# Token rows stored as 16-bit halves and transposed by their load DMAs, in a mixture-of-experts kernel

## The chip, the core and the metric

The kernel runs on one core of a Trainium2 chip. The metric is the time of one execution in microseconds (us) of device time; the median of several executions counts. TensorE (PE) multiplies matrices out of the on-chip memory SBUF into the accumulator memory PSUM, in tiles of 128 partitions. VectorE (DVE), ScalarE (ACT) and GpSimd (POOL) do the elementwise work; SyncE (SP) here issues DMAs, and GpSimd issues the indirect ones, which scatter rows to addresses that a table holds. Sixteen DMA engines serve all queues. Engines run side by side, each through its own list of instructions in order, and wait for each other by semaphores.

## What is computed

x has 2 x 1024 tokens of 256 values. The first half of the reference is a cross attention in three rounds with the tokens as slots; the second is a mixture of experts with routing, and the change lies there:

```python
x = x + _L0_xcond_ref(cond_1024, ctx_1024, _layernorm(x), ...)
x = x + _L0_ffn_ref(_layernorm(x), ...)

# _L0_ffn_ref: E = 32 experts, H = 256, I = 128, TOPK = 8
scores = jax.nn.sigmoid(h @ gate_w.T)
# the 8 best experts of 4 of 8 groups, weights normalised and scaled by 2.5
combine = (jax.nn.one_hot(tki, E) * tkw[..., None]).sum(1)
g = jax.nn.silu(jnp.einsum('th,eih->tei', h, w_gate))
u = jnp.einsum('th,eih->tei', h, w_up)
routed = jnp.einsum('tei,ehi->th', g * u * combine[:, :, None], w_down)
shared = jax.nn.silu(h @ sh_gate.T) * (h @ sh_up.T) @ sh_down.T
return (routed + shared)
```

All values are float32.

## The kernel before

The 2048 tokens are four blocks of 512 (numbers 0 to 3), each four tiles of 128. The attention rounds of the four blocks are interleaved by an order written out by hand for each engine. After the third round of a block, the layernorm of its tokens (`normalise(i, 2 * ROUNDS, xs)` on ScalarE) writes the normalised rows into `slots`, the first 256 words of each row of `tokrow`. TensorE transposes them (`transpose_block`), ScalarE copies the result (`copy_tokens`), TensorE makes the gate's logits, and ScalarE the sigmoid (`score_tokens`). VectorE chooses experts, and finds a place in the DRAM table `xrows` for each pair of token and expert.

A row of `tokrow` and of `xrows` has 320 words: 256 of the token, 32 weights and 32 destinations. GpSimd dispatches it: `dispatch(i, step)` issues two indirect DMAs, each 128 rows, so 32 for a block, 128 in all. The rows of an expert lie one behind the other, filled up with rows of zeros (`padrow`), and are then worked in `TILES` = 159 tiles of 128 rows, in three phases (33, 30 and 96 tiles) as the blocks' routing is known.

The expert loop, tile n:
- SyncE loads the 128 rows of 1280 bytes into one of 12 buffers `rowbuf` (places in `hat` and `rows`), L485. From tile 12 to 43 a write of zeros for an expert's end stands behind each load. It waits until the buffer's last tile is turned (`row_turned`) and its weights are picked (`own_ready`).
- TensorE transposes the row tile in two halves of 128 columns into PSUM (`turn_row`, whose `transpose` is recorded at L1882), ScalarE copies it to `turned_row` (`copy_row`, L1446).
- TensorE multiplies gate and up (L2023; a float32 matmul is two records), ScalarE does silu (L1453), VectorE the product (L1267), TensorE transposes it (L2036), VectorE copies it back (L1274; from tile 116 ScalarE, L1462), TensorE multiplies down (L2043), and ScalarE writes the result, scaled by the row's weight, to one of 48 and then 41 buffers (`copy_out`, L1470).
- GpSimd scatters the results to `yrows` (L704). In its list 32 steps of `dispatch` for blocks 2 and 3 (64 DMAs) come first, and a scatter behind each from the 13th on. The last six tiles are not scattered but added by a matmul (L2075).

TensorE's list has, in iteration n of the loop: row transposes of tile n, gate/up of n - 1, transpose of the product of n - 2, down of n - 3.

Results come back by `ask_back(g)`, a load of 1 MB for each of 16 token tiles, on SyncE's queue: number 0 behind the row load of tile 128, when scatters 0 to 95 have landed, others at places written out in `ASK_AT`, and numbers 12 to 14 when scatter 152 has landed, 15 also when the last tile is done. VectorE adds the eight results of a token tile to `xs`, the first of them in iteration 120 (`SUM_AT`), each sum standing in its list in front of later products.

Of the kernel before, what the change touches and what calls it, by code (L numbers as in the profile page):

```python
# [6 lines left out]
I32 = mybir.dt.int32  # L7
ALU = mybir.AluOpType
ACT = mybir.ActivationFunctionType
# [87 lines left out]
def build(nc, x, ctx_in, rows_in, bias_in, cols_in, mats_in, gate_wT, experts, out, xrows, yrows):  # L97
    with ExitStack() as stack:
# [152 lines left out]
        picked = part(mats[:, 4, :, :], GROUP * E, GROUP * 2, E)  # L251
        rowgroup = [part((hat, rows)[i // 2][:, :, :], i % 2 * GROUP * ROW, GROUP, ROW) for i in range(ROWBUFS // GROUP)]
# [60 lines left out]
        row_turned, row_copied, gate_up_done, silu_done = sem("row_turned"), sem("row_copied"), sem("gate_up"), sem("silu_done")  # L313
# [62 lines left out]
        def sync_program():  # L376
# [89 lines left out]
            for n in range(TILES):  # L466
# [44 lines left out]
        def gpsimd_program():  # L511
# [89 lines left out]
            def dispatch(i, step):  # L601

                if step == 0:
                    gp.wait_ge(placed, i + 1)
                    gp.wait_ge(weighed, 2 * (i + 1))
                    gp.wait_ge(normed[i // Q], past(i, 2 * ROUNDS, TQ))
                g = i * TQ + step // 4
                for k in (2 * (step % 4), 2 * (step % 4) + 1):
                    gp.indirect_dma_start(  # L609
                        out=xrows[:, :], out_offset=bass.IndirectOffsetOnAxis(ap=place_of[:, g, k:k + 1], axis=0),  # L610
                        in_=tokrow[:, g, :], in_offset=None).then_inc(dispatched[i], 16)
# [108 lines left out]
        def vector_program():  # L720
# [523 lines left out]
            def pick(m):  # L1244
                for n in range(m * GROUP, (m + 1) * GROUP):
                    ve.wait_ge(row_in[n % ROWBUFS], 16 * (n // ROWBUFS + 1))
# [110 lines left out]
            for g in range(EARLY_SUMS, EARLY_SUMS + TQ):  # L1357
                y = last_back if g == EARLY_SUMS + 3 else back[g % 3]
                if y is last_back:
                    ve.wait_ge(row_in[0], 16 * (-(-TILES // ROWBUFS) + 1))  # L1360
# [12 lines left out]
        def scalar_program():  # L1373
# [205 lines left out]
            score_tokens(0)  # L1579
            evacuate(3, 3)  # L1580
# [8 lines left out]
            score_tokens(1)  # L1589
            normalise(3, 4, slots)  # L1590
# [16 lines left out]
            score_tokens(2)  # L1607
# [512 lines left out]
```

## Time and profile before

| | us |
|---|---|
| median of 3 runs | 613.6 |
| lowest, highest | 612.79, 614.25 |
| the profiled execution, its own time | 612.29 |
| its span, first to last instruction | 611.0 |
| the expert loop within the span | about 331 to 595 |

The profile is of one execution. "Busy" is the time in which an engine has an instruction in work; records of TensorE overlap, since the next matmul starts before the last has drained. An idle time is put down to the instruction that ended it; "issue" means that nothing in the profile was waited for. The chain that ended last is followed back from the end, at each step to what released it. The DMA share is the mean busy share of the 16 engines. "hardware_dynamic" q1 is SyncE's queue, "software_dynamic" q0 GpSimd's.

### The profile page before, as it was taken

How to read it: one execution, taken by the hardware profiler on the slowest of the kernel's cores; microseconds unless marked ns; L12 is line 12 of the kernel's file. 1: busy time of each engine (PE TensorE's matmuls, PEld its weight loads, DVE VectorE, ACT ScalarE, POOL GpSimd, SP SyncE). 2: the span in 40 equal slices, each digit the busy share in tenths (PEclk: the TensorE clock that was granted, in tenths of full speed). 3: DMA queues.
4: the chain of work that ended last, by engine and by line, in shares of the span. 5: the costliest groups of instructions: out<-in, count | busy, mean ns of one | idle time of the engine just before them, and what ended most of it. 6: DMA issues, size and time to landing. Idle time of an engine off the chain costs nothing.

```text
span 611.0 us, 11524 instructions
## 1 busy us (share of the span) xinstructions
PE 563.9 (92%) x2677; PEld 422.3 (69%) x2677; DVE 407.4 (67%) x1554; ACT 372.3 (61%) x993; POOL 361.8 (59%) x414
## 2 busy tenths in 40 slices
PE   3989989889999798798997999999999999999996
PEld 2666557655766455555666888888788888888875
DVE  6975675986768987647776444444444444688897
ACT  1867888868786755552611666566566666677760
POOL 4343233632143377876777777777777777777730
PEclk9979999999999899899799999999999999999999
DMA  8999300000000023239364999876666666999966
GB/s 258 394 397 383 131 0 2 1 1 0 2 0 0 17 92 119 98 119 343 119 222 167 304 321 342 293 223 214 200 202 205 209 207 198 346 412 407 411 255 222
DMA packets 62063, 119.69 MB, mean 196 GB/s; under 512 B 8667, under 2 KB 45583, under 8 KB 59951
## 3 DMA queue, kind: packets, MB, share of 16 engines
q1 hardware_dynamic: 48079, 77.63, 37.5%
q0 software_dynamic: 13488, 41.04, 17.7%
q8 instruction: 25, 0.41, 0.3%
q10 hardware_dynamic: 432, 0.29, 0.3%
q14 instruction: 39, 0.32, 0.2%
HBM read 61.29 MB, written 57.64 MB: 195 GB/s over the span
## 4 chain that ended last, share of the span: by engine, by line
PE 78%; DVE 10%; ACT 6%; DMA 3%; issue 1%; POOL 1%; SPq 0%; DVEq 0%; POOLq 0%; ACTq 0%
PE ps L2023 22%; PE ps L2043 11%; PE ps L1671 7%; PE ps L1656 6%; PE ps L1882 5%; PE ps L1682 5%; PE ps L1695 5%; PE ps L2036 3%; PE ps L1642 3%; PE ps L1777 3%; PE ps L1783 2%; DVE tokrow L750 2%; PE ps L1794 2%; DMA arena<-yrows 2%; DMA xs<-in_x 1%
## 5 line engine op out<-in xcount | busy, mean ns | idle before, releaser
L2023 PE MATMUL ps<-arena,mats 128*128 x636 | 164.0, 381 | 0.3 <-issue 0.3
L609 POOL DMA_INDIRECT xrows<-tokrow,place_of x128 | 125.2, 978 | 41.8 <-issue 37.5
L1267 DVE TENSOR_TENSOR mats<-ps,mats 128x128 f32<-128x128 f32 x159 | 46.3, 291 | 106.1 <-ACT mats L1453 101.1
L2023 PEld LDWEIGHTS ps<-arena,mats 128*128 128x128 f32 x636 | 108.6, 191 | 8.8 <-issue 0.5
L2043 PE MATMUL ps<-arena,mats 128*128 x318 | 95.5, 383 | 1.0 <-DVE mats L1274 1.0
L1453 ACT ACTIVATE mats<-ps 128x128 f32<-128x128 f32 x159 | 44.1, 277 | 56.4 <-PE ps L2023 56.4
L1446 ACT COPY mats<-ps 128x256 f32<-128x256 f32 x159 | 58.0, 365 | 11.9 <-PE ps L1882 11.9
L1387 ACT ACTIVATE hat<-tokrow,total 128x256 f32<-128x256 f32 x96 | 47.6, 499 | 18.8 <-DVE tokrow L815 11.7
L1395 ACT ACTIVATE hat<-tokrow,shift,rstd 128x256 f32<-128x256 f32 x96 | 49.7, 591 | 12.9 <-POOL shift L540 12.8
L2043 PEld LDWEIGHTS ps<-arena,mats 128*128 128x128 f32 x318 | 48.0, 191 | 13.7 <-issue 2.1
L545 POOL TENSOR_SCALAR var_eps<-variance 128x4 f32<-128x4 f32 x24 | 6.4, 269 | 83.5 <-ACT hat L1387 83.2
L704 POOL DMA_INDIRECT yrows<-hatT,mats x48 | 46.1, 961 | 14.6 <-issue 11.0
L1682 PE MATMUL ps<-hatT,arena 128*128 128x512 f32 x96 | 47.2, 638 | 4.3 <-ACT hatT L1402 4.3
L1695 PE MATMUL ps<-mats,hat 128*128 128x256 f32 x192 | 44.4, 384 | 4.5 <-ACT hat L1422 4.5
L1671 PE MATMUL ps<-arena 128*128 128x257 f32 x192 | 45.6, 393 | 0.1
L1695 PEld LDWEIGHTS ps<-mats,hat 128*128 128x128 f32 x192 | 35.6, 190 | 13.7 <-ACT hat L1422 4.8
L1656 PE MATMUL ps<-hatT,arena 128*128 128x512 f32 x96 | 43.1, 596 | 2.1 <-ACT hatT L1402 2.1
L2036 PE MATMUL ps<-ident,mats 128*128 128x128 f32 x159 | 43.6, 274 | 1.6 <-DVE mats L1267 1.4
L704 POOL DMA_INDIRECT yrows<-tokrow,mats x38 | 38.0, 999 | 11.6 <-issue 8.5
L1671 PEld LDWEIGHTS ps<-arena 128*128 128x128 f32 x192 | 37.1, 197 | 7.2 <-DVE arena L804 1.2
L1682 PEld LDWEIGHTS ps<-hatT,arena 128*128 128x128 f32 x96 | 19.3, 205 | 26.2 <-issue 20.4
L536 POOL TENSOR_TENSOR rstd<-var_eps,minus_half 128x4 f32<-128x4 f32 x16 | 18.6, 1160 | 29.1 <-DVE var_eps L740 29.0
(237 smaller groups left out, 1136.0 us busy)
## 6 DMA issues: line engine op xcount, KB each, us to landing
hat<-xrows SPq DMA_DIRECT2D x81, 160.0 KB
rows<-xrows SPq DMA_DIRECT2D x78, 160.0 KB
arena<-in_experts SPq DMA_DIRECT2D x4, 1920.0 KB, 18.8
xrows<-padrow SPq DMA_DIRECT2D x32, 160.0 KB
hat<-yrows SPq DMA_DIRECT2D x5, 1024.0 KB, 8.4
tokrow<-yrows SPq DMA_DIRECT2D x5, 1024.0 KB
hatT<-yrows SPq DMA_DIRECT2D x5, 1024.0 KB, 8.9
xrows<-padrow SPq DMA_DIRECT2D x1, 4960.0 KB
```

Of the source, the lines that this page charges most:

```text
L609: gp.indirect_dma_start(out=xrows[:, :], out_offset=bass.IndirectOffsetOnAxis(ap=place_of[:, g, k:k + 1], axis=0), in_=tokrow[:, g, :], in ...
L704: gp.indirect_dma_start(out=yrows[:, :], out_offset=bass.IndirectOffsetOnAxis(ap=scatter_to[:, n:n + 1], axis=0), in_=ybuf[y_place(n)], in ...
L1387: it = ac.activation(hat[:, g, :], slots[:, g, :], ACT.Square, bias=total[:, g:g + 1], scale=-float(D), accum_out=variance[:, g:g + 1])
L1395: ac.activation(into[:, g, :], source[:, g, :], ACT.Identity, bias=shift[:, g:g + 1], scale=rstd[:, g:g + 1]).then_inc(normed[i // Q], 1)
L1446: ac.copy(turned_row[u], bank(4 + u)[:, 0:D]).then_inc(row_copied, 1)
L1656: mm = te.matmul(bank(banks_of(i)[h]), kq[:, dc, j * NH:j * NH + P], hatT[b][:, dc, span_of(i)], start=dc == 0, stop=dc == DC - 1)
L1671: mm = te.matmul(bank(banks_of(i)[k])[:, 0:D + 1], attn[b][:, h, t * P:(t + 1) * P], vscaled[b][:, h, 0:D + 1], start=h == 0, stop=h == 1)
L1682: mm = te.matmul(bank(banks_of(i)[fc]), w1g[:, dc, fc * P:(fc + 1) * P], hatT[b][:, dc, span_of(i)], start=dc == 0, stop=dc == DC - 1)
L1695: mm = te.matmul(bank(banks_of(i)[k])[:, t * D:(t + 1) * D], gel[i][:, fc, s:s + P], mat("w2", fc), start=fc == 0, stop=fc == DC - 1)
L2023: mm = te.matmul(bank(6 + u)[:, 0:2 * I], turned_row[u][:, dc * P:(dc + 1) * P], arena[:, dc * D:(E - 1) * WCOL + (dc + 1) * D][:, bass.ds ...
L2036: te.transpose(bank(u)[:, 0:I], act[u], ident[:, :]).then_inc(act_turned, 1)
L2043: te.matmul(bank(2 + u)[:, 0:D], actT[u], arena[:, 2 * D:(E - 1) * WCOL + 3 * D][:, bass.ds(at, D)], start=True, stop=True).then_inc(down_ ...
```

## The change

Rows in `xrows` hold the same 1280 bytes, but a token's 256 words are stored as 256 low 16-bit halves followed by 256 high halves. `normalise` now writes the tokens' layernorm into `hat`, from where TensorE transposes them for the gate, and a new ScalarE copy per block, `halve(i)`, over 128 x 2048 halves, writes them split into `slots`. The dispatch waits for it, and so does the shared experts' silu of the block, whose buffer lies in `hat`.

A tile's load is two DMAs: a transposing DMA of 128 rows by 512 halves, which leaves the halves of column c of each block of 128 on partition c, and a plain one of the 64 words behind them. `turn_row` is gone; `copy_row` reads the transposed halves from `rowbuf` and interleaves them into the words of `turned_row`. A buffer is free once `copy_row` has read it. The rest of the diff, not shown, puts the wait for the tables into `gate_up`, names `hat` as source of the other blocks' `transpose_block`, adds `halve(2)` and `halve(3)` in the same way, and adapts the counts of semaphores to two DMAs.

```diff
+        halves, whole_rows = xrows.bitcast(HALF), xrows.bitcast(I32)
+        rowhalf = [buf[:, 0:D].bitcast(HALF).rearrange("p (c r) -> p c r", c=2 * DC) for buf in rowbuf]
...
                 if n >= ROWBUFS:
-                    sy.wait_ge(row_turned, n - ROWBUFS + 1)
+                    sy.wait_ge(row_copied, n - ROWBUFS + 1)
                     sy.wait_ge(own_ready, (n - ROWBUFS) // GROUP + 1)
-                sy.dma_start(rowbuf[n % ROWBUFS], xrows[bass.ds(at[n % 4], P), :]).then_inc(row_in[n % ROWBUFS], 16)
+                sy.dma_start_transpose(rowhalf[n % ROWBUFS], halves[bass.ds(at[n % 4], P), 0:2 * D]
+                                       ).then_inc(row_in[n % ROWBUFS], 16)
+                sy.dma_start(rowbuf[n % ROWBUFS][:, WTS:ROW], xrows[bass.ds(at[n % 4], P), WTS:ROW]
+                             ).then_inc(row_in[n % ROWBUFS], 16)
...
-                    gp.wait_ge(normed[i // Q], past(i, 2 * ROUNDS, TQ))
+                    gp.wait_ge(halved, i + 1)
...
-                into = hat if n < 2 * ROUNDS else slots
                 for g in tiles_of(i):
-                    ac.activation(into[:, g, :], source[:, g, :], ACT.Identity, bias=shift[:, g:g + 1],
+                    ac.activation(hat[:, g, :], source[:, g, :], ACT.Identity, bias=shift[:, g:g + 1],
...
+            def halve(i):
+                ac.wait_ge(normed[i // Q], past(i, 2 * ROUNDS, TQ))
+                ac.copy(slots[:, set_of(i), :].bitcast(HALF).rearrange("p t (h d) -> p t h d", h=2),
+                        hat[:, set_of(i), :].bitcast(HALF).rearrange("p t (d h) -> p t h d", h=2)).then_inc(halved, 1)
+
             def shared_silu(i, u):
                 ac.wait_ge(sh_gate, i * SHARED + u + 1)
+                ac.wait_ge(halved, i + 1)
...
             def copy_row(s):
                 u = s % 2
-                ac.wait_ge(row_turned, s + 1)
+                ac.wait_ge(row_in[s % ROWBUFS], 32 * (s // ROWBUFS + 1))
                 if s >= 2:
                     ac.wait_ge(gate_up_done, s - 1)
-                ac.copy(turned_row[u], bank(4 + u)[:, 0:D]).then_inc(row_copied, 1)
+                ac.copy(turned_row[u].bitcast(HALF).rearrange("p (n h) -> p h n", h=2),
+                        rowhalf[s % ROWBUFS].rearrange("p (h c) r -> p h (c r)", h=2)).then_inc(row_copied, 1)
...
-            def turn_row(s):
-                u = s % 2
-                te.wait_ge(row_in[s % ROWBUFS], 16 * (s // ROWBUFS + 1))
...
             for n in range(TILES + 3):
-                if 1 <= n < TILES:
-                    turn_row(n)
```

TensorE in the expert loop, one tile, before (`mats` holds `turned_row` and the products, `arena` the experts' weights, `ps` is PSUM, `ident` the identity; an ISA row sets an address from a register):

```order
L2036 MATMUL ps<-ident,mats 128x128 [waits actT_ready,act_ready]
L2043 ISA [waits y_ready,actT_ready]
L2043 MATMUL ps<-arena,mats 128x256
L1882 MATMUL ps<-ident,hat 128x128 [waits row_copied,row_in3]
L1882 MATMUL ps<-ident,hat 128x128
L2023 ISA [waits act_ready,row_copied]
L2023 MATMUL ps<-arena,mats 128x256
L2023 ISA
L2023 MATMUL ps<-arena,mats 128x256
```

and after:

```order
L2040 MATMUL ps<-ident,mats 128x128 [waits actT_ready,act_ready]
L2047 ISA [waits y_ready,actT_ready]
L2047 MATMUL ps<-arena,mats 128x256
L2027 ISA [waits act_ready,row_copied]
L2027 MATMUL ps<-arena,mats 128x256
L2027 ISA
L2027 MATMUL ps<-arena,mats 128x256
```

The two L1882 rows of a tile are gone, and with them the wait for the loaded row; the transpose of the product is L2040 now, the gate/up matmuls L2027, down L2047.

ScalarE from the sigmoid of block 1's scores on, before (`mats` holds the scores):

```order
L1433 ACTIVATE mats<-ps 128x128 [waits gate_sum]
L1395 ACTIVATE hat<-tokrow,shift,rstd 128x256 [waits shift1]
L1395 ACTIVATE hat<-tokrow,shift,rstd 128x256 x3
L1402 COPY hatT<-ps 128x512 [waits turned1] x2
L1439 ACT_TABLE_LOAD
L1439 ACTIVATE hat<-ps 128x512 [waits sh_gate]
L1412 ACT_TABLE_LOAD
L1412 ACTIVATE arena,rowsum<-ps,expbias 77x512 [waits bias1] x4
```

and after:

```order
L1438 ACTIVATE mats<-ps 128x128 [waits gate_sum]
L1444 COPY tokrow<-hat 128x4x512 [waits normed0]
L1400 ACTIVATE hat<-tokrow,shift,rstd 128x256 [waits shift1]
L1400 ACTIVATE hat<-tokrow,shift,rstd 128x256 x3
L1407 COPY hatT<-ps 128x512 [waits turned1] x2
L1450 ACT_TABLE_LOAD [waits halved]
L1450 ACTIVATE hat<-ps 128x512 [waits sh_gate]
L1417 ACT_TABLE_LOAD
```

A copy of 128 x 4 x 512 halves (L1444) stands between the sigmoid and the next layernorm, and the load of the silu's table behind it waits for it.

SyncE in the stretch with writes of zeros, one tile and the start of the next, before:

```order
L485 ISA [waits own,row_turned]
L485 DMA hat<-xrows 128x320
L495 ISA
L495 DMA xrows<-padrow 128x320
L485 ISA [waits own,row_turned]
L485 DMA rows<-xrows 128x320
```

and after:

```order
L488 ISA [waits own,row_copied]
L488 DMA_TRANSPOSE hat<-xrows 128x4x128
L490 ISA
L490 DMA hat<-xrows 128x64
L501 ISA
L501 DMA xrows<-padrow 128x320
L488 ISA [waits own,row_copied]
```

Each tile has one more load in the list, ahead of the write of zeros, and the load waits for ScalarE's copy instead of TensorE's transposes.

## Rows read from the trace of the kernel before

**Rows 1.** The page, part 1 (busy us, share, instructions) and part 4 (chain by engine).
```profile
PE 563.9 (92%) x2677; PEld 422.3 (69%) x2677; DVE 407.4 (67%) x1554; ACT 372.3 (61%) x993; POOL 361.8 (59%) x414
...
PE 78%; DVE 10%; ACT 6%; DMA 3%; issue 1%; POOL 1%; SPq 0%; DVEq 0%; POOLq 0%; ACTq 0%
```

**Rows 2.** Order of time, TensorE, a tile (start us, duration us, line, operation).
```profile
460.26 0.38 PE L1882 MATMUL ps<-ident,rows 128*128 128x128 f32 x2
460.48 1.03 PE L2023 MATMUL ps<-arena,mats 128*128 x4
461.34 0.27 PE L2036 MATMUL ps<-ident,mats 128*128 128x128 f32 x1
461.45 0.60 PE L2043 MATMUL ps<-arena,mats 128*128 x2
461.88 0.38 PE L1882 MATMUL ps<-ident,rows 128*128 128x128 f32 x2
```

**Rows 3.** Busy by stretch: each engine's us and count, clock, DMA share, GB/s.
```profile
400.00:510.00 110.00, 109.51 (x606) 92.31 (x605) 52.44 (x224) 68.04 (x202) 83.49 (x87) 1.00 0.67 207
...
540.00:570.00 30.00, 30.00 (x168) 25.41 (x167) 25.47 (x74) 21.64 (x75) 23.30 (x22) 1.00 1.04 408
...
331.00:595.00 264.00, 261.13 (x1430) 218.70 (x1430) 153.77 (x564) 167.74 (x518) 196.06 (x200) 1.00 0.80 276
```

**Rows 4.** Order of time: GpSimd's scatters 0, 20, 95, 152; then ScalarE's result of tile 152.
```profile
342.61 0.96 POOL L704 DMA_INDIRECT yrows<-hatT,mats  x1 [0.30 <-issue]
...
416.14 0.96 POOL L704 DMA_INDIRECT yrows<-tokrow,mats  x1 [0.30 <-ACT hatT L1470]
...
511.27 0.99 POOL L704 DMA_INDIRECT yrows<-hatT,mats  x1 [0.30 <-issue]
...
586.95 0.97 POOL L704 DMA_INDIRECT yrows<-tokrow,mats  x1 [0.30 <-issue]
...
585.85 0.47 ACT L1470 ACTIVATE tokrow<-ps,mats 128x256 f32<-128x256 f32 x1
```

**Rows 5.** Groups by form, ScalarE copies: count, busy us, mean ns, idle before.
```profile
L1446 ACT COPY mats<-ps 128x256 f32<-128x256 f32 x159 | 58.0, 365 | 11.9 <-PE ps L1882 11.9
...
L1402 ACT COPY hatT<-ps 128x512 f32<-128x512 f32 x48 | 25.5, 585 | 14.5 <-PE ps L1642 14.4
...
L1462 ACT COPY mats<-ps 128x128 f32<-128x128 f32 x43 | 11.2, 261 | 0.5 <-PE ps L2036 0.5
```

**Rows 6.** Order of time around the first two sigmoids (L1433): ScalarE, TensorE, VectorE.
```profile
201.63 1.07 ACT L1402 COPY hatT<-ps 128x512 f32<-128x512 f32 x2
...
202.76 5.40 PE L1682 MATMUL ps<-hatT,arena 128*128 128x512 f32 x8 [1.33 <-ACT hatT L1402]
...
209.26 0.29 DVE L916 TENSOR_TENSOR mats<-ps,mats 128x128 f32<-128x128 f32 x1
...
228.92 2.07 ACT L1395 ACTIVATE hat<-tokrow,shift,rstd 128x256 f32<-128x256 f32 x4 [0.17 <-POOL shift L540]
...
231.68 1.04 PE L1642 MATMUL ps<-ident,hat 128*128 128x128 f32 x8
```

**Rows 7.** Order of time: first fetch of results, the tail's first and last, VectorE's use.
```profile
521.65 0.38 SPq L456 DMA_DIRECT2D hat<-yrows  x1
...
589.58 0.32 SPq L456 DMA_DIRECT2D hat<-yrows  x1
...
595.00 0.32 SPq L452 DMA_DIRECT2D arena<-yrows  x1
...
604.33 1.29 DVE L1297 TENSOR_TENSOR arena<-arena 128x512 f32<-128x512 f32 x2 [0.44 <-DMA arena<-yrows]
```

**Rows 8.** DMA queues in 460 to 500 us, then 595 to 611: packets, MB, share.
```profile
q1 hardware_dynamic: 3482, 3.97, 38.9%
...
q0 software_dynamic: 1511, 4.10, 26.8%
...
q1 hardware_dynamic: 1442, 3.69, 63.0%
```

More of the change, by code:

```diff
@@ L7 @@
 I32 = mybir.dt.int32
+HALF = mybir.dt.uint16
 ALU = mybir.AluOpType
@@ L609, in dispatch @@
                     gp.indirect_dma_start(
-                        out=xrows[:, :], out_offset=bass.IndirectOffsetOnAxis(ap=place_of[:, g, k:k + 1], axis=0),
-                        in_=tokrow[:, g, :], in_offset=None).then_inc(dispatched[i], 16)
+                        out=whole_rows[:, :], out_offset=bass.IndirectOffsetOnAxis(ap=place_of[:, g, k:k + 1], axis=0),
+                        in_=tokrow[:, g, :].bitcast(I32), in_offset=None).then_inc(dispatched[i], 16)
             context_rstd()
@@ L1245, in pick @@
                 for n in range(m * GROUP, (m + 1) * GROUP):
-                    ve.wait_ge(row_in[n % ROWBUFS], 16 * (n // ROWBUFS + 1))
+                    ve.wait_ge(row_in[n % ROWBUFS], 32 * (n // ROWBUFS + 1))
                 ve.wait_ge(matched, m + 1)
@@ L1359, in vector_program @@
                 if y is last_back:
-                    ve.wait_ge(row_in[0], 16 * (-(-TILES // ROWBUFS) + 1))
+                    ve.wait_ge(row_in[0], 32 * -(-TILES // ROWBUFS) + 16)
                 else:
@@ L1579, in scalar_program @@
             score_tokens(0)
+            halve(0)
             evacuate(3, 3)
@@ L1589, in scalar_program @@
             score_tokens(1)
+            halve(1)
             normalise(3, 4, slots)
@@ L1607, in scalar_program @@
             score_tokens(2)
+            halve(2)
             normalise(3, 2 * ROUNDS, xs)
@@ L1611, in scalar_program @@
             score_tokens(3)
+            halve(3)
             shared_silu(2, 1)
@@ L1871, in transpose_slots @@
                 transpose_block(i, n, hat)
-            def turn_row(s):
-                u = s % 2
-                te.wait_ge(row_in[s % ROWBUFS], 16 * (s // ROWBUFS + 1))
-                if s < 2:
-                    te.wait_ge(tables_ready, 3 * (s + 2))
-                if s >= 2:
-                    te.wait_ge(row_copied, s - 1)
-                for dc in range(DC):
-                    tr = te.transpose(bank(4 + u)[:, dc * P:(dc + 1) * P], rowbuf[s % ROWBUFS][:, dc * P:(dc + 1) * P],
-                                      ident[:, :])
-                tr.then_inc(row_turned, 1)
             turn_context()
@@ L1964, in tensor_program @@
             transpose_slots(3, 3)
-            transpose_block(0, 2 * ROUNDS, slots)
+            transpose_block(0, 2 * ROUNDS, hat)
             gate_logits(0)
@@ L1972, in tensor_program @@
             logits(2, 2)
-            transpose_block(1, 2 * ROUNDS, slots)
+            transpose_block(1, 2 * ROUNDS, hat)
             gate_logits(1)
@@ L1995, in tensor_program @@
             shared_down(1)
-            transpose_block(2, 2 * ROUNDS, slots)
+            transpose_block(2, 2 * ROUNDS, hat)
             gate_logits(2)
             shared_gate_up(2, 0)
-            transpose_block(3, 2 * ROUNDS, slots)
+            transpose_block(3, 2 * ROUNDS, hat)
             rank(2)
@@ L2012, in tensor_program @@
             sum_runs(2)
-            turn_row(0)
             spread_runs(2)
@@ L2018, in gate_up @@
                 u = s % 2
+                if s < 2:
+                    te.wait_ge(tables_ready, 3 * (s + 2))
                 te.wait_ge(row_copied, s + 1)
```

2 lines of the change are left out of this document (1 added, 1 removed).

## The prediction

> **What bounds the kernel now.** I read the page first: TensorE is busy 92% of the span and holds 78% of the chain that ended last, GpSimd only 59% [rows 1]. That looks like a kernel in which every TensorE cycle taken away is time won. The order of time says what one tile of the expert loop costs TensorE: from one pair of row transposes to the next 1.62 us, and from the pair to the first gate/up matmul behind it 0.22 us [rows 2]. So the two transposes are worth 0.22 us, not the 0.38 us that their record shows: starts follow each other before the ends.
>
> The second thing to see is a queue that the chain does not name. GpSimd issues one indirect DMA after another: 0.96 us for one and 0.30 us of issue before it, whatever it would have waited for [rows 4]. Scatter 20 starts at 416.14 and scatter 152 at 586.95: 132 of them in 170.8 us, 1.294 us each, with never more than the issue gap. The last one starts 0.6 us after ScalarE has written its tile (585.85 + 0.47) [rows 4]. GpSimd began the loop with a backlog of 64 dispatches and has just worked it off when TensorE gets to the end. Two limits, one hidden behind the other, end within 1 us. The stores of the first three quarters, and the fetch at 589.58 that opens the tail [rows 7], need its last scatter.
>
> The third is the DMA engines: over the loop, 331 to 595 us, they are busy 0.80 of the time, 0.67 in the middle and full between 540 and 570 [rows 3].
>
> **TensorE.** 159 pairs go: 159 x 0.22 = 35 us less work, 1.40 us a tile. Its granted clock, 1.00 in all stretches while it is busy [rows 3], is no term. On the path almost nothing of it is left:
> - The first fetch of results needs scatter 95. It starts at 511.27, and a scatter is in memory 1.7 us after its 0.99 us (586.95 + 0.97 to the fetch at 589.58). So that fetch can go at 513.9 instead of 521.65 [rows 4, 7], and lands some 7 to 9 us later. VectorE's first sum is written in front of the product of tile 120, so TensorE, which would be there at 331 + 120 x 1.40 = 499, stands until about 522. Some 21 of the 26 us won by then are given back at one place.
> - The last three fetches need scatter 152, which does not move: it is the 132nd behind scatter 20 as before. So 589.58 stays, apart from a shift of GpSimd's start.
> - The very last fetch (595.00) waits for the last tile instead of the scatters. It can go right behind the other three. VectorE waited 0.44 us for it [rows 7]: gain 0.4 us.
>
> **ScalarE in the loop.** The copy of a turned row reads 512 halves where it read 256 words. Its rows: 128 columns 261 ns, 512 columns 585 ns [rows 5], 0.844 ns a column. I take 585 ns, 0.22 more than the 365 ns now; the bounds are 0.365 (it goes by bytes) and 1.02 (a two-byte element in steps of two takes twice as long). ScalarE's work for a tile is 68.04 of 110 us, 1.01 us, and in the late stretch with a second copy 21.64 of 30, 1.17 us [rows 3]; with 0.22 it is 1.23 and 1.39, under TensorE's 1.40. It costs nothing; without that cover it would cost the excess over 1.62 us. VectorE waits for rows 12 tiles ahead, as before.
>
> **ScalarE before the loop.** Four new copies of 2048 halves: 585 + 1536 x 0.844 = 1.9 us each; bounds 1.0 by bytes and about 3.7. All stand behind a sigmoid.
> - The first pushes the copy at 201.63 for which TensorE already waited 1.33 us; its work behind that feeds VectorE's L916 at 209.26 [rows 6], which is in VectorE's unbroken chain of routing. I allow 0.6 us of slack: 1.3 us on the path.
> - The second pushes the normalisation of 228.92, whose fourth tile would come at 232.9 instead of 231.0; TensorE turns those tiles from 231.68 to 232.72 [rows 6]: 0.8 us.
> - Behind the third and fourth, TensorE has shared-expert matmuls in hand; nothing, or 1.9 each if that cover is gone.
> Sum 2.1 us, bounds 0 and 7.5. GpSimd waits for the same steps before its unbroken run, so its run moves too. The wait of the dispatch on the halves adds nothing: its places are known later.
>
> **The loads.** They have no row of their own, so they are bounded. In 460 to 500 us the row queue moved 3482 packets of 1140 bytes in 38.9% of 16 engines, 71.5 ns each; in 595 to 611, 1442 of 2559 bytes in 63.0%, 112 ns [rows 8]. The line through both gives 39 ns + 0.0285 ns a byte, so 46 ns for 256 bytes. A row load is now 0.389 x 1.627 = 0.63 us of all engines, 142 packets.
> - The plain 256 bytes per row: 142 x 46 / 16 = 0.41 us; by bytes alone 0.13.
> - The transposed 1024 bytes per row: by bytes 0.63 x 128/160 = 0.50 us. The other end: it is written as four column blocks, and if each row of each block is a packet of 256 bytes, 512 x 46 / 16 = 1.48 us.
> Extra per tile: 0.0 at the least, 0.50 + 0.41 - 0.63 = 0.28, at the most 1.26. The room: 0.20 of 264 us is 53 us, 0.33 a tile [rows 3]. I take 0.28, because the bytes of both loads are the row load's own and it is issued by the same queue; it is close to the edge. Where the engines are full, 540 to 570, 18 tiles x 0.28 = 5 us must move into neighbours. Loads run 12 tiles ahead, so I put 1.0 us for it (0 to 5). SyncE issues two loads of some 0.35 us [rows 7] where it issued one, within 1.4 us.
>
> On this price the Trainium skill leans to the low end: "DMA: Bandwidth & Descriptors", section "Latency and other measured facts", gives transposing DMAs with a middle dimension that is not contiguous 261 GB/s, by which 131 KB would be an estimated 0.50 us. No row here shows it; with the packet price instead, the sum is the second rival's.
>
> **The sum.** Profiled execution 612.3; + 2.1 - 0.4 + 1.0 = 615.0. It ran 1.3 us under the median of 613.6, so 616.3. Its own range, with the bounds above: 612.6 to 625.
>
> **Rivals.**
> - *The loads pace the loop.* If a 256-byte piece pays a packet, the engines have 211 + 159 x 1.26 = 411 us of work for 264: + 147, 763 us. Half of that extra (0.8) gives 338, + 74, 690 us. A second way to the same side: transposing loads of one queue do not overlap; then a load takes 0.50 + 1.7 us, 2.2 a tile, 159 x 0.58 = + 92, 708 us. For it: pieces of 256 bytes and two-byte elements, no row of which exists. It decides from 0.33 us extra a tile. Chance 0.42, of which 0.08 lies beyond 763. The Trainium skill speaks for it in "VectorE: DVE Perf Modes", section "The three transpose paths": one 128x128 block of two-byte data takes the DMA path 1309 ns; four in a row would be an estimated 5.2 us a tile and over 1100 us in all. No row shows whether such blocks overlap.
> - *Not slower.* GpSimd's run ends earlier, since its operations are no longer stretched: 132 x (1.294 - 1.266) = 3.7 us, once loads and fetches do not meet as they do now, and ScalarE's copies are absorbed. 613.6 - 3.7 - 0.4 = 609.5. It decides as soon as the copies put less than 4 us on the path. Against it: the fetches start earlier and the engines get more work. Chance 0.07.
> - *ScalarE becomes the bound.* With 1.02 us for the copy it has 1.66 us a tile for 116 tiles and 1.82 for 43: the loop ends at 602 instead of 595, and the early copies cost double: + 11, 625 us. Chance 0.05.
>
> **How the numbers follow.** My case (0.46) is likeliest: 616.3. About 0.2%, 1.2 us, is what a measurement here can tell from no change. Of my case 0.13 lies within that (copies mostly absorbed) and 0.33 above. So faster 0.07, same 0.13, slower 0.33 + 0.42 + 0.05 = 0.80. The range takes in my case, ScalarE's and the loads' up to 763: 612.5 to 763, leaving out 0.07 below and 0.08 above.
>
> **What would show it.** TensorE's tile at 1.40 us between about 345 and 500, then a stop near tile 120 until about 522; GpSimd's scatters still 1.27 to 1.3 us apart and the last near 589; four ScalarE copies of about 1.9 us and 159 of about 0.59 us; in the middle a DMA share of about 0.91/1.40 for loads and 0.27 for scatters, 0.92 together, instead of 0.67. If the copy of a row waits for its load from tile to tile and the DMA share is near 1 throughout, the loads pace the loop and 616 is wrong. If the last scatter starts before 585, the limit on GpSimd was misread.

## The result, and the profile after

The changed kernel takes 734.4 us (median of 4 runs, 728.8 to 737.1) where the kernel before, on the same chip, takes 613.9 (612.8 to 616.1): 1.195 times the time, 95% interval 1.186 to 1.203. The sign was as forecast and the time lies in the range (612.5 to 763), but only because the range took in a rival: the predicted time, 616.3, is off by 118 us. The rival "the loads pace the loop" happened, though by neither of the two mechanisms under it.

The page of the kernel after, parts 1 and 4, beside [rows 1]:

```profile
span 735.1 us, 11062 instructions
...
PE 589.9 (80%) x2359; PEld 410.1 (56%) x2359; DVE 404.5 (55%) x1554; ACT 425.7 (58%) x997; POOL 359.7 (49%) x414
...
SPq 36%; PE 34%; DVE 8%; issue 7%; ACT 7%; DMA 6%; POOL 2%; DVEq 0%; ACTq 0%; POOLq 0%
SPq L488 22%; SPq L490 9%; PE ps L1687 6%; PE ps L1672 6%; PE ps L1698 5%; PE ps L1711 4%; PE ps L1658 2%; PE ps L2027 2%; PE ps L1793 2%; ACT hat L1400 2%; PE ps L2047 2%; SPq L501 2%; SPq L482 2%; DMA tokrow<-yrows 2%; DVE tokrow L756 1%
```

No arithmetic engine is near its limit. What leads the chain is SPq, SyncE's own queue of instructions: 36% of the span, and nearly all of it issuing loads (L488 transposing, L490 plain; L501 pad rows, L482 the register load of four addresses). In the profile before, SPq had 0% of the chain. The order of time of SyncE in the middle of the loop (start us, duration us) shows the pace:

```profile
499.25 1.24 SPq L488 DMA_TRANSPOSE hat<-xrows  x1
500.69 0.42 SPq L490 DMA_DIRECT2D hat<-xrows  x1
501.31 1.20 SPq L488 DMA_TRANSPOSE hat<-xrows  x1
502.71 0.41 SPq L490 DMA_DIRECT2D hat<-xrows  x1
503.64 1.20 SPq L488 DMA_TRANSPOSE hat<-xrows  x1
...
510.07 1.20 SPq L488 DMA_TRANSPOSE hat<-xrows  x1
```

The issue of a transposing load holds SyncE for 1.20 us, that of the plain one for 0.42, with 0.2 between them, and 0.5 ahead of every second tile (at every fourth the register load L482 stands there): five tiles in 10.82 us (499.25 to 510.07), 2.16 each, where TensorE's pace was 1.62 [rows 2]. SyncE waits for nobody while it does so. Its waits (line, what it waited for, us in total, times, longest), first before, then after:

```profile
SPq L484 <- DVE mats L1257: 60.5, 37, 14.5
SPq L485 <- PE ps L1882: 48.2, 65, 1.1
```

```profile
SPq L433 <- PE ps L1698: 222.1, 2, 210.8
SPq L472 <- DMA xrows<-tokrow,place_of: 35.6, 1, 35.6
SPq L464 <- DVE xs L1332: 12.4, 2, 12.2
SPq L458 <- DMA yrows<-tokrow,mats: 12.4, 1, 12.4
```

Before, SyncE stood some 109 us in front of the loads of the loop, because no row buffer was free: it was 12 tiles ahead. After, those two waits are gone. What is left lies ahead of the loop (L433, L472) and around the last loads (L458, L464). In the middle of the loop the DMA engines are not full either. Busy by stretch after (engines' us, clock, DMA share, GB/s):

```profile
450.00:500.00 50.00, 40.54 (x167) 29.06 (x165) 17.25 (x75) 31.18 (x74) 23.60 (x25) 0.93 0.62 139
500.00:550.00 50.00, 40.02 (x161) 28.87 (x162) 18.07 (x80) 29.20 (x68) 21.09 (x22) 0.93 0.54 134
550.00:600.00 50.00, 40.00 (x158) 28.95 (x157) 17.03 (x76) 28.98 (x68) 22.25 (x23) 0.90 0.57 139
...
650.00:700.00 50.00, 36.04 (x136) 26.66 (x137) 27.89 (x79) 28.55 (x77) 18.52 (x19) 0.86 1.06 255
```

The last row is the stretch of the fetches. The engines are full there as they were before (1.04 [rows 3]), but move 255 GB/s instead of 408. Issues last longer in it: the longest of a transposing load takes 2.79 us, and from 610 to 700 us all issues of loads together hold SyncE some 5.5 us more than at their usual times. So in this stretch the engines have a part in the loss.

Where the time goes is read from ScalarE's copies of the rows of tiles 43, 120 and 158 in the order of time, before and after:

```profile
401.40 0.36 ACT L1446 COPY mats<-ps 128x256 f32<-128x256 f32 x1
527.56 0.36 ACT L1446 COPY mats<-ps 128x256 f32<-128x256 f32 x1
590.73 0.36 ACT L1446 COPY mats<-ps 128x256 f32<-128x256 f32 x1
```

```profile
444.83 0.75 ACT L1457 COPY mats<-rows 128x512 uint16<-128x512 uint16 x1
610.11 0.75 ACT L1457 COPY mats<-hat 128x512 uint16<-128x512 uint16 x1
714.94 0.75 ACT L1457 COPY mats<-hat 128x512 uint16<-128x512 uint16 x1
```

Up to tile 43 the kernel after is 43.4 us late, 37.1 of it behind tile 12, where SyncE issues a pad row with each load. From 43 to 120 another 39.1 (165.3 against 126.2 us for 77 tiles), from 120 to 158 another 41.7 (104.83 against 63.17), and behind the last copy nothing (20.2 against 20.3). The last third costs 1.1 us a tile instead of 0.5. SyncE issues the fetches of results there too, and a fetch stands behind loads that are late: the first, behind the load of tile 128, is issued at 624.11, when ScalarE had copied the row of tile 120 at 610.11 (before, the fetch went out at 521.65 and that copy came at 527.56). VectorE stands for it, and TensorE for VectorE; this one stop, between tiles 120 and 123, makes 18 of the 41.7 us:

```profile
624.11 0.33 SPq L459 DMA_DIRECT2D hat<-yrows  x1
...
629.74 1.29 DVE L1303 TENSOR_TENSOR hat<-hat 128x512 f32<-128x512 f32 x2 [14.69 <-DMA hat<-yrows]
```

### The profile page after: what moved, and what is told of

Same layout as the page of the kernel before. It is cut to its first block, busy times and chain, and to the rows that moved or that the text cites. A ratio compares the mean times of both kernels' runs of the same rounds, so it can differ in the third digit from the quotient of the medians.

```text
span 735.1 us, 11062 instructions
## 1 busy us (share of the span) xinstructions
PE 589.9 (80%) x2359; PEld 410.1 (56%) x2359; DVE 404.5 (55%) x1554; ACT 425.7 (58%) x997; POOL 359.7 (49%) x414
## 3 DMA queue, kind: packets, MB, share of 16 engines
q1 hardware_dynamic: 134575, 77.65, 39.0%
## 4 chain that ended last, share of the span: by engine, by line
SPq 36%; PE 34%; DVE 8%; issue 7%; ACT 7%; DMA 6%; POOL 2%; DVEq 0%; ACTq 0%; POOLq 0%
SPq L488 22%; SPq L490 9%; PE ps L1687 6%; PE ps L1672 6%; PE ps L1698 5%; PE ps L1711 4%; PE ps L1658 2%; PE ps L2027 2%; PE ps L1793 2%; ACT hat L1400 2%; PE ps L2047 2%; SPq L501 2%; SPq L482 2%; DMA tokrow<-yrows 2%; DVE tokrow L756 1%
## 5 line engine op out<-in xcount | busy, mean ns | idle before, releaser
L2027 PE MATMUL ps<-arena,mats 128*128 x636 | 189.1, 424 | 1.0 <-issue 0.9
L2027 PEld LDWEIGHTS ps<-arena,mats 128*128 128x128 f32 x636 | 126.8, 211 | 41.1 <-issue 19.0
L615 POOL DMA_INDIRECT xrows<-tokrow,place_of x128 | 125.2, 978 | 42.8 <-issue 37.5
L2040 PE MATMUL ps<-ident,mats 128*128 128x128 f32 x159 | 49.6, 312 | 93.2 <-DVE mats L1273 93.0
L2047 PE MATMUL ps<-arena,mats 128*128 x318 | 112.7, 441 | 3.9 <-DVE mats L1280 3.8
L2040 PEld LDWEIGHTS ps<-ident,mats 128*128 128x128 f32 x159 | 24.6, 155 | 114.6 <-DVE mats L1273 110.0
L710 POOL DMA_INDIRECT yrows<-hatT,mats x48 | 46.1, 961 | 44.2 <-ACT hatT L1482 37.5
L2047 PEld LDWEIGHTS ps<-arena,mats 128*128 128x128 f32 x318 | 54.8, 216 | 21.0 <-issue 9.8
L1457 ACT COPY mats<-hat 128x512 uint16<-128x512 uint16 x81 | 61.0, 755 | 0.0
L1457 ACT COPY mats<-rows 128x512 uint16<-128x512 uint16 x78 | 58.8, 754 | 1.4 <-DMA rows<-xrows 1.4
L1698 PE MATMUL ps<-hatT,arena 128*128 128x512 f32 x96 | 47.7, 644 | 6.2 <-ACT hatT L1407 6.2
L1672 PE MATMUL ps<-hatT,arena 128*128 128x512 f32 x96 | 46.5, 634 | 2.1 <-ACT hatT L1407 2.1
L1482 ACT ACTIVATE hatT<-ps,mats 128x256 f32<-128x256 f32 x48 | 22.7, 473 | 37.6 <-PE ps L2047 35.5
L710 POOL DMA_INDIRECT yrows<-shared,mats x24 | 23.4, 974 | 41.5 <-ACT shared L1482 35.4
```

The costliest lines, as they stand in the source:

```text
L615: gp.indirect_dma_start(out=whole_rows[:, :], out_offset=bass.IndirectOffsetOnAxis(ap=place_of[:, g, k:k + 1], axis=0), in_=tokrow[:, g, : ...
L710: gp.indirect_dma_start(out=yrows[:, :], out_offset=bass.IndirectOffsetOnAxis(ap=scatter_to[:, n:n + 1], axis=0), in_=ybuf[y_place(n)], in ...
L1457: ac.copy(turned_row[u].bitcast(HALF).rearrange("p (n h) -> p h n", h=2), rowhalf[s % ROWBUFS].rearrange("p (h c) r -> p h (c r)", h=2)).t ...
L1672: mm = te.matmul(bank(banks_of(i)[h]), kq[:, dc, j * NH:j * NH + P], hatT[b][:, dc, span_of(i)], start=dc == 0, stop=dc == DC - 1)
L1698: mm = te.matmul(bank(banks_of(i)[fc]), w1g[:, dc, fc * P:(fc + 1) * P], hatT[b][:, dc, span_of(i)], start=dc == 0, stop=dc == DC - 1)
L2027: mm = te.matmul(bank(6 + u)[:, 0:2 * I], turned_row[u][:, dc * P:(dc + 1) * P], arena[:, dc * D:(E - 1) * WCOL + (dc + 1) * D][:, bass.ds ...
```

## The experiments

Theory S: the time that SyncE needs to issue a transposing DMA paces the loop. Rival D: the DMA engines need the time, for pieces of 256 bytes. Rival L: transposing loads do not overlap. Rival A: ScalarE's longer copies. Beside these stands the forecast's claim that GpSimd hides what TensorE gains.

One thing is needed to read the numbers. On the chips of the first eight runs the kernel before itself took 718 us: between some 200 and 480 us the engines stood still again and again there (behind 500 us a tile takes 1.67 us, near the usual 1.62). Those runs are compared with the kernels before and after on such chips alone, 718 and 818 us. The last four ran where the kernel before takes 615.

**One load at a time, on an idle chip.** At the very end of the kernel before, behind its last store, series of loads issued by SyncE:

```diff
+            series(sy, 1, 4)
+            series(sy, 6, 4)
+            series(sy, 6, 2)
+            series(sy, 6, 1)
+            series(sy, 6, 0)
...
```

The first number is how many loads, the second how many blocks of 128 halves each one turns; with 0 they are plain ones of 64 words a row. `series` waits until all have landed. Six plain loads of 320 words follow.

> The kernel before, unchanged, with series of loads at its very end, when every engine is idle, all issued by SyncE: one transposing load of 128 rows by 512 halves; six of them; six of 256 halves; six of 128 halves; six plain loads of 64 words a row; six plain ones of 320 words. Theory S: the issue of a 512-half one takes 1.2 us on an idle chip as well, the six start 1.4 us apart, and those of 256 and 128 halves take less in proportion if it goes by pieces (about 0.75 and 0.5). Rival L: six land one behind the other, each 2.5 us or more behind the one ahead. Rival D: the first issue is short (0.35 us) and only later ones, behind a full ring, are long. The time of the whole kernel: 613 us plus some 35 to 50.

Measured, the instructions of the series by line (count: ns min/median/max, first and last start in us), L519 transposing, L522 plain:

```profile
L519 SPq DMA_TRANSPOSE hat<-xrows x16: 1129/1236/1322, 720.0 to 745.9; - x16
L519 SPq DMA_TRANSPOSE rows<-xrows x3: 1232/1241/1269, 729.2 to 747.2; - x3
L522 SPq DMA_DIRECT2D hat<-xrows x5: 373/432/432, 749.6 to 751.4; - x5
```

The order of time of SyncE: the very first load, and where the series of 512 halves ends and that of 256 begins:

```profile
719.95 1.32 SPq L519 DMA_TRANSPOSE hat<-xrows  x1
...
727.95 1.26 SPq L519 DMA_TRANSPOSE hat<-xrows  x1
729.25 1.27 SPq L519 DMA_TRANSPOSE rows<-xrows  x1
731.92 1.17 SPq L519 DMA_TRANSPOSE hat<-xrows  x1
```

And busy by stretch (the last two columns are the DMA share and GB/s), one row for each series of six (transposing 512, 256 and 128 halves, plain 64 and 320 words):

```profile
722.60:730.50 7.90, 0.00 (x0) 0.00 (x0) 0.00 (x0) 0.00 (x0) 0.00 (x0) 0.50 0.37 83
731.90:739.80 7.90, 0.00 (x0) 0.00 (x0) 0.00 (x0) 0.00 (x0) 0.00 (x0) 0.50 0.19 43
740.90:748.40 7.50, 0.00 (x0) 0.00 (x0) 0.00 (x0) 0.00 (x0) 0.00 (x0) 0.50 0.10 22
749.60:752.40 2.80, 0.00 (x0) 0.00 (x0) 0.00 (x0) 0.00 (x0) 0.00 (x0) 0.50 0.21 47
753.70:756.50 2.80, 0.00 (x0) 0.00 (x0) 0.00 (x0) 0.00 (x0) 0.00 (x0) 0.50 0.59 171
```

The issue takes 1.24 us with nothing else on the chip, whether 512, 256 or 128 halves a row are turned; a plain one takes 0.43, of 64 or of 320 words. The first load, with nothing queued ahead of it, takes 1.32 us, so the time is not that of a full ring, as D would have it. The issues follow each other after 1.30 us (727.95, 729.25), while the last of a series has landed 2.7 us behind its own start (729.25 to 731.92). So they overlap, against L. The engines are busy 0.37 of the time under an unbroken stream of the widest ones, against D too. What S had expected of the narrower ones, less time in proportion, was wrong: the issue has a fixed price.

**Half the pieces.** The load turns two of the four column blocks:

```diff
-                sy.dma_start_transpose(rowhalf[n % ROWBUFS], halves[bass.ds(at[n % 4], P), 0:2 * D]
+                sy.dma_start_transpose(rowhalf[n % ROWBUFS][:, DC:2 * DC, :], halves[bass.ds(at[n % 4], P), D:2 * D]
```

> The kernel after with two of the four column blocks transposed (the upper halves of the words; the lower halves are not loaded after the change, which is left out work): half the pieces of the transposing load. Theory S with an issue time that grows with the pieces: 0.65 to 0.8 us for one issue instead of 1.2, SyncE's period about 1.5 to 1.65 us a tile, 625 to 650 us. Theory S with a fixed issue time: 1.2 us, 734 us as before. Rival D (the DMA engines need the time for the pieces, the issue only reflects a full ring): issue time falls with the engines' busy share, from 0.6 to about 0.4 in the middle of the loop.

Measured 817.6 us (4 runs), the kernel after on such a chip 817.9. The issue of its loads in the loop (ns min/median/max), and a stretch of the middle:

```profile
L488 SPq DMA_TRANSPOSE hat<-xrows x81: 17/1181/2182, 329.4 to 776.4; - x81
```

```profile
550.00:600.00 50.00, 40.57 (x165) 29.17 (x165) 18.29 (x80) 30.00 (x69) 22.38 (x24) 0.93 0.39 109
```

The minimum of 17 ns is a record whose time stands on the register operation ahead of it. Half the transposing work, engines at 0.39 instead of the 0.54 of the kernel after on such a chip in the same stretch, and nothing won that the spread of the runs would show: D falls as the pace of the loop, and the fixed price is confirmed inside it.

**The plain loads on another queue.** ScalarE issues them from tile 12 on, SyncE keeps the transposing ones; the work of the DMA engines is the same:

```diff
-                sy.dma_start(rowbuf[n % ROWBUFS][:, WTS:ROW], ...
+                if n < TAIL_LEAD:
+                    sy.dma_start(rowbuf[n % ROWBUFS][:, WTS:ROW], ...
...
+                ac.wait_ge(own_ready, (n - ROWBUFS) // GROUP + 1)
+                ac.dma_start(rowbuf[n % ROWBUFS][:, WTS:ROW], xrows[bass.ds(tail_at[n % 4], P), WTS:ROW]
+                             ).then_inc(row_in[n % ROWBUFS], 16)
```

> The kernel after with the plain 64-word loads issued by ScalarE from tile 12 on, nine tiles ahead, instead of SyncE; the result is the same. SyncE keeps only the transposing loads. Theory S: SyncE's period falls from 2.1 to about 1.5 us a tile; ScalarE gets some 0.3 to 0.5 us of issuing on top of 1.4 us of work a tile, so it becomes the pacer at 1.7 to 1.9 us: 650 to 690 us. Rival D (the DMA engines' 256-byte pieces) and rival L (transposing loads follow each other only as they land): the engines have the same work, so 725 to 740 us as before.

> The kernel of c_tails_scalar once more (plain loads issued by ScalarE from tile 12 on). Theory S: SyncE's transposing loads alone take 1.2 us of issue and 0.25 us around it, and ScalarE with its added issuing makes 1.65 to 1.75 us a tile (the first run showed about 1.7 in its undisturbed stretch): 640 to 665 us. Rivals D and L (DMA engines' pieces, serial landing): 725 to 740 us.

> The kernel of c_tails_scalar on a chip where the kernel before is hoped to take 613 to 616 us, as it did for the last three kernels. Theory S: SyncE's transposing loads alone (1.2 us and some 0.2 between, a register load every fourth tile) allow 1.5 us a tile, under TensorE's old pace; ScalarE with its copy of 0.76 us and its added issuing makes 1.65 to 1.75 us a tile: 635 to 660 us. Rivals D and L (the DMA engines' pieces, serial landing): 725 to 740 us. Where the kernel before takes 718 us: 745 us again.

Measured 749.4 and 745.4 us beside 718; and 653.4 us (6 runs, 649.2 to 655.4) beside 614.9, 1.062 times (1.058 to 1.066). Of the 120 us that the change costs, 82 come back when 0.6 us a tile is taken off SyncE. This is the verdict for S, inside the loop, with the result unchanged. It also shows how near the DMA engines are to being the next limit. In the middle their share is now 0.97 (and 0.84 from 500 to 550 us), where the slower loop of after had 0.62:

```profile
450.00:500.00 50.00, 45.60 (x204) 32.68 (x203) 22.66 (x96) 39.57 (x88) 38.11 (x40) 1.00 0.97 211
```

ScalarE in the middle of the third of these runs (start us, us, line; ACTq is its queue issuing), and its row copies of tiles 43, 120 and 158:

```profile
501.20 0.76 ACT L1459 COPY mats<-rows 128x512 uint16<-128x512 uint16 x1
501.83 0.26 ACT L1467 ACTIVATE mats<-ps 128x128 f32<-128x128 f32 x1
502.00 0.47 ACT L1484 ACTIVATE block_sum<-ps,mats 128x256 f32<-128x256 f32 x1
502.15 0.35 ACTq L1643 DMA_DIRECT2D hat<-xrows  x1
502.60 0.77 ACT L1459 COPY mats<-rows 128x512 uint16<-128x512 uint16 x1
...
419.46 0.77 ACT L1459 COPY mats<-rows 128x512 uint16<-128x512 uint16 x1
552.27 0.76 ACT L1459 COPY mats<-hat 128x512 uint16<-128x512 uint16 x1 [0.73 <-PE ps L2050]
630.68 0.76 ACT L1459 COPY mats<-hat 128x512 uint16<-128x512 uint16 x1
```

Where the rest lies (39.9 us between the two profiled spans): 18.1 up to tile 43, with the pad rows still on SyncE's queue behind each transposing load; 6.6 from 43 to 120, at 1.72 us a tile, nearly all of it ScalarE's (0.77 + 0.26 + 0.47 us at work and 0.35 of issuing, partly beside it; SyncE is 12 tiles ahead again from tile 88 on); 15.2 from 120 to 158, where SyncE issues the fetches as well, the engines are full and the longest issue of a transposing load takes 3.54 us. What of this last part is the engines' and what is SyncE's was not separated.

**All but the transposition.** The columns come by a plain DMA, the rest is the kernel after:

```diff
-                sy.dma_start_transpose(rowhalf[n % ROWBUFS], halves[bass.ds(at[n % 4], P), 0:2 * D]
+                sy.dma_start(rowbuf[n % ROWBUFS][:, 0:D].bitcast(I32), whole_rows[bass.ds(at[n % 4], P), 0:D]
```

> The kernel after with one thing undone: the 512 columns of a row load come by a plain DMA instead of a transposing one (ScalarE copies the same number of halves in the same pattern; left out is the transposition itself, so the experts see rows that are not turned). Two loads per tile, their bytes, the halves before the loop, ScalarE's 0.755 us copy and TensorE without row transposes all stay. Theory S (SyncE's issue time of the transposing DMA, 1.2 us, paces the loop): the two plain issues take 0.35 to 0.45 us each, some 1.0 us a tile, SyncE waits for buffers again, and the loop is GpSimd's once more: 615 to 624 us. Rival A (ScalarE's longer copy and its work before the loop hold the loop): stays above 680. Rival 'two loads instead of one' (whatever their kind): 680 or more.

> The kernel of a_plain_pair once more (two plain loads, the rest as after), because in its first batch every kernel, the one before too (718 us), stood still for stretches of up to 31 us between 350 and 480 us that have no counterpart in the earlier traces. Theory S (SyncE's issue time of the transposing DMA): 615 to 624 us where the kernel before takes 613. Rival A (ScalarE's 0.755 us copy and its work before the loop): above 680.

Measured 734.9 and 736.4 us beside 718, 1.021 and 1.020 times (the second: 1.012 to 1.029), where after has 1.140. So 82 of the 99 us that the change costs on those chips are the transposing DMA's own. The 17 that remain are more than S had said, 2 to 11. The kernel with its plain pair was not run on a chip where before takes 615, so what part of the 17 belongs to those chips alone stays open. The rows' copies say where they lie: against those of the next kernel, from the same chip, this one is 4.1 us later at tile 43, 5.4 at 120, 12.8 at 124 and 16.3 at 158. So about half is one stop, where VectorE waits 6.0 us for the first fetch of results. What made the fetch late was not tested; the next three kernels bound the other parts.

**The work before the loop.** The front of after with the loop of before. Its copies also write with a stride, so that the result stays right:

```diff
+                ac.copy(slots[:, set_of(i), :].bitcast(HALF).rearrange("p t (d h) -> p t h d", h=2),
+                        hat[:, set_of(i), :].bitcast(HALF).rearrange("p t (d h) -> p t h d", h=2)).then_inc(scored, 1)
```

> The loop of the kernel before (one plain load, TensorE's row transposes, ScalarE's 0.365 us copy) behind the front of the kernel after (ScalarE's four copies of 2048 halves, the last normalisation into the other tile, the dispatch that waits for the copies). The copies read and write the words in place, so the result is the reference's. It prices the work before the loop by itself: by the trace of after, where the start of the loop was 4.6 to 5.8 us later, 617 to 620 us; by the forecast, 615.7; if the shift of after came from elsewhere (TensorE's lower clock), 613 to 615.

Measured 722.8 us (10 runs) beside 718.4: 1.005 times (1.001 to 1.009), so 4.4 us, 0.9 to 6.3. Its copies took 2.46 us each, not after's 1.89, so this is rather the upper end. The last table of addresses gives the same in other traces: VectorE writes it at 330.1 before, at 332.7 in the last run of the kernel with ScalarE's loads, which has the same front as after, and at 336.0 after; the three kernels of the last chips with an unchanged front showed 329.9 to 332.1. So 2 to 3 us can be put down to the front; the other 3 of after's 5.8 have no cause that a run shows, and unchanged fronts alone differ by 2.2.

**TensorE without its row transposes.** The kernel before, with the copy reading the loaded row:

```diff
-                    turn_row(n)
...
-                ac.copy(turned_row[u], bank(4 + u)[:, 0:D]).then_inc(row_copied, 1)
+                ac.copy(turned_row[u], rowbuf[s % ROWBUFS][:, 0:D]).then_inc(row_copied, 1)
```

> The kernel before without TensorE's 318 row transposes: ScalarE copies the loaded columns as they are (256 words, 0.37 us), so the experts see rows that are not turned, which is the part left out. One plain load a tile, nothing new before the loop. It prices the gain that the change could bring at most. The forecast's claim (GpSimd's unbroken run of indirect DMAs hides all of TensorE's 35 us): the same time within 1 us of the kernel before, where that takes 613 us. Rival (TensorE holds the path): 576 to 590 us against 613. Where the kernel before takes 718 us, its engines stand still so often that GpSimd has no unbroken run: then 5 to 35 us less than 718 would say only that TensorE's work counts there.

Measured 615.0 us (10 runs) beside 615.8: 0.997 times (0.994 to 1.001). So what the change takes off TensorE wins nothing that the runs show, by the interval at most 3.7 us. The trace shows how it is lost: TensorE's tile takes 1.44 us from tile 60 to 120, and then VectorE stands for the first fetch, and TensorE for VectorE, until 520; the last scatter starts at 588.83. The order of time:

```profile
519.64 1.29 DVE L1297 TENSOR_TENSOR hat<-hat 128x512 f32<-128x512 f32 x2 [12.34 <-DMA hat<-yrows]
...
588.83 0.96 POOL L704 DMA_INDIRECT yrows<-tokrow,mats  x1 [0.31 <-issue]
```

**GpSimd a little slower.** A small memset ahead of each scatter of the kernel before:

```diff
+                gp.memset(spare[:, :], 0.0).then_inc(pool_seq, 1)
+                gp.wait_ge(pool_seq, seq.add())
                 gp.indirect_dma_start(
```

> The kernel before with one small memset (48 words in each of 128 partitions) and the wait for it on GpSimd ahead of each of the 159 scatters: some 0.1 to 0.2 us of GpSimd's time each. If GpSimd's unbroken run is the second limit of the loop, as the forecast read from the trace, the 132 scatters from 20 to 152 take 13 to 26 us more and the kernel 10 to 25 us more where it takes 613 us. Rival (only TensorE counts, GpSimd has slack): no more than 2 us. Where the kernel before takes 718 us GpSimd has gaps, and the effect should be under 5 us.

Measured 636.5 us beside 615.8, 1.031 times (1.026 to 1.035). The order of time of GpSimd has the scatters 1.40 us apart instead of 1.27; scatter 152, at 586.95 in [rows 4], starts 26.0 us later, and the kernel takes 20.7 us more:

```profile
451.43 0.97 POOL L707 DMA_INDIRECT yrows<-hat,mats  x1 [0.28 <-POOL spare L705]
452.39 0.15 POOL L705 MEMSET spare<- 128x48 f32 x1
452.83 0.97 POOL L707 DMA_INDIRECT yrows<-hat,mats  x1 [0.28 <-POOL spare L705]
...
612.95 0.97 POOL L707 DMA_INDIRECT yrows<-tokrow,mats  x1 [0.28 <-POOL spare L705]
```

An engine busy 59% of the span is on the path, which the chain of waits, 78% TensorE and 1% GpSimd [rows 1], does not show.

**ScalarE's longer copy alone.** The kernel before, the row copy by halves with a stride of two:

```diff
+                ac.copy(turned_row[u].bitcast(HALF).rearrange("p (n h) -> p h n", h=2),
+                        bank(4 + u)[:, 0:D].bitcast(HALF).rearrange("p (n h) -> p h n", h=2)).then_inc(row_copied, 1)
```

> The kernel before with one thing changed: ScalarE's copy of a turned row moves the same bytes as 512 halves with a stride of two instead of 256 words; the result is the reference's. It prices ScalarE's longer copy alone: 0.75 us instead of 0.365, 61 us more work over 159 tiles. If the slack of the loop hides it (forecast; ScalarE then works 1.4 us of a tile's 1.6): within 2 us of the kernel before. If it counts, because ScalarE's instructions for a tile follow each other through TensorE (copy, gate/up, activation): up to 0.1 us a tile, 5 to 17 us more, which would account for what a_plain_pair took beyond e_halves_only (13 us).

Measured 614.3 us (10 runs) beside 615.8: 0.997 times (0.994 to 1.000).

```profile
L1447 ACT COPY mats<-ps 128x512 uint16<-128x512 uint16 x159 | 115.4, 726 | 11.5 <-PE ps L1884 11.5
```

57 us more work on ScalarE, and none of it counts: rival A falls for this kernel's order of work.

**The control.** The kernel after unchanged, on a chip of the first kind:

> The kernel after, unchanged, as the control on this chip: 729 to 737 us where the kernel before takes 613 us. If the kernel before is again above 700 us here, the ratio of the two tells whether the disturbance adds to the change or hides it: added, 830 us; hidden, 750 or less.

Measured 817.9 us (4 runs) beside 718.4: 1.140 times, 99 us more. Neither of the two expected cases is met; the disturbance adds 84 us to after and 105 to before, so it hides a part of the change's cost but not most of it.

## Why the prediction was right and wrong

- **The step that failed** stands at the end of "The loads": "SyncE issues two loads of some 0.35 us [rows 7] where it issued one, within 1.4 us." The 0.35 was the issue of a plain fetch, and it was given to the transposing DMA as if an issue cost the same whatever is issued. No row of before showed one. Unlike the engines' time for the loads, this term got one value and no bounds. It measures 1.21 us in the loop and 1.24 alone. The sum for SyncE is then 1.20 + 0.42 + 0.4 of gaps, with the longer gap at every second tile 2.16 us a tile, 0.54 over TensorE's 1.62. Over 159 tiles that is an estimated 86 us of the 120. The rest lies where the stages show it: 6.3 us are there by tile 12, SyncE issues pad rows up to tile 43, and behind tile 120 stand the stop for the first fetch and the full engines. The runs do not divide it further.
- **The rival had the right place and the wrong reason,** and that the measured time lies in the range is owed to it: luck, not a mechanism that was seen. It priced the DMA engines (690 and 763 us). As the pace of the loop this is refuted by the share of 0.54 to 0.62, by half the pieces at the same time, and by the engines' share on the idle chip; it holds in part behind 640 us, where the engines are full. The sign given for it, a DMA share near 1 throughout, did not show, and still the loads pace the loop. Its other way, loads that do not overlap (2.2 us a tile, 708 us), has nearly the measured pace by chance; the loads do overlap.
- **The engines' time for the loads** was forecast at 0.28 us more a tile (0.0 to 1.26). On the idle chip 131 KB at 83 GB/s take 1.58 us at a share of 0.37, 0.58 us of all engines; the plain 64 words 0.15 (32.8 KB at 47 GB/s, 0.21); the old load 0.57 (164 KB at 171 GB/s, 0.59). That is 0.16 more. In the kernel it is 0.36: the row queue's share is 39.0% of 735.1 us against 37.5% of 611.0. The second is more than the 0.33 of room that the prediction counted. At SyncE's pace the engines had room in the middle, but with ScalarE's loads, at 1.72 us a tile, their share is already 0.97; whether they would have carried the forecast's 1.40 is not shown. By the 261 GB/s that the Trainium skill states in "DMA: Bandwidth & Descriptors", section "Latency and other measured facts", 131 KB were an estimated 0.50 us; the measured 0.58 is near it, and neither is the time of the queue.
- **"Four in a row", 5.2 us a tile**, the estimate from the 1309 ns for one block in "VectorE: DVE Perf Modes", section "The three transpose paths", of the Trainium skill, did not come: four blocks in one DMA have landed after 2.7 us, one after 2.4 us at most (747.19 to 749.57), and such loads overlap.
- **Two slips in the sums.** With its own bounds the range of the case forecast is 613.2 to 625.7, not 612.6 to 625. And half of the extra of 1.26 is 0.63, not 0.8; with it the rival's lower price is some 663 us, not 690. Neither touches the step that failed.
- **GpSimd's bound** was right, and the two kernels that test it are the ones closest to their numbers: TensorE at 1.44 us a tile for 1.40, the stop near tile 120 until 520 for 522, the last scatter at 588.83 for 589, and + 20.7 us for 10 to 25. In the kernel after none of this is seen, because GpSimd's unbroken run is itself broken: it waits for ScalarE's results, and those for the loads. The page of after (count, busy us, mean ns, idle before and for whom):

```profile
L1457 ACT COPY mats<-hat 128x512 uint16<-128x512 uint16 x81 | 61.0, 755 | 0.0
L710 POOL DMA_INDIRECT yrows<-hatT,mats x48 | 46.1, 961 | 44.2 <-ACT hatT L1482 37.5
```

- **ScalarE.** The copies before the loop: 1.89 us each, forecast 1.9; their price on the path 2.1, measured 2 to 3 by the table's time and at most 6.3. The row copy: 0.755 us by the row above, forecast 0.585. The line through two f32 rows did not hold for halves written with a stride. That error cost nothing in the kernel before, as the run with the longer copy shows.
- **TensorE's clock**, no term of the sum, reads 0.90 to 0.93 from 450 to 600 us of after, where TensorE is busy 40 of 50 us, and the gate/up matmuls take 424 ns instead of 381 on average. The granted clock is a mean of its two levels there, 1.2 and 2.4 GHz. It was at 1.00, the upper level throughout, from 450 to 550 us of the run with ScalarE's loads, where TensorE is busy 46 of 50. That it follows from the waits and does not make them is a reading; no run tests it by itself.

## What to carry to other kernels

Price a DMA three times: on the queue that issues it, on the engines that move it, and from issue to landing. A queue that stands idle for 109 us because its buffers are full is slack that one slow instruction a tile can use up, and nothing in the old profile tells the price of an instruction of a new kind: give it bounds, however small its neighbours are. And before work is taken off the busiest engine, look for the engine that never waits for more than its own issue gap: here taking 35 us off TensorE alone was worth nothing that could be measured.

## What the runs showed of the hardware

- Issuing a transposing DMA of 16-bit data holds SyncE 1.2 us, on an idle chip and in the loop, and the same for 128, 256 and 512 columns of 128 rows; a plain one 0.33 to 0.43. To turn four times the columns with one instruction costs the queue nothing more. Where the DMA engines are full (share 1.06 and more) single issues took up to 2.79 us in the kernel after and 3.54 with ScalarE's loads.
- ScalarE's queue issues a plain 32 KB load in 0.34 us, and part of this lies beside its running activation (502.15, while L1484 runs from 502.00 for 0.47 us).
- ScalarE copies 128x512 halves to a stride of two in 0.755 us from SBUF, 0.726 from PSUM when both sides have the stride; 128x2048 take 1.89 us when the read side alone has the stride and 2.46 when both have it. So it is the strided write that costs, 0.57 us for 2048 halves.
- The turned rows appear in the packets of the row queue: 134575 instead of 48079, 544 more a tile.
- On some chips the same kernel takes 718 us instead of 614, in every run. The engines stand still again and again between 200 and 480 us, where GpSimd's dispatches run; the longest wait of ScalarE in the profile with the series of loads was 31 us (released by "remote"). What holds them was not found.
